# Masking the first attention with a matmul: the bf16 mask product on TensorE, maximum and difference read straight from PSUM

## The chip, the cores and the metric

One core of one Trainium2 chip runs the whole program. The metric is the device time of one execution in microseconds (us), the median of several runs. Below, TensorE is PE (PEld is its weight load), VectorE is DVE, ScalarE is ACT, GpSimd is POOL and the sync engine's queue is SP.

## What is computed

Four layers, each an attention onto a short context and a feed-forward part, both with a layernorm ahead and a tanh gate behind. The change touches only the first attention:

```python
qh, kh, vh = heads_split(q @ Wq), heads_split(k @ Wk), heads_split(v @ Wv)    # 16 heads of 64
dots = jnp.einsum('bhid,bhjd->bhij', qh, kh) * scale
dots = jnp.where(mask[:, None, :, :], -jnp.finfo(dots.dtype).max, dots)
attn = jax.nn.softmax(dots, axis=-1)
out = jnp.einsum('bhij,bhjd->bhid', attn, vh)
x = x + tanh(g) * (out.transpose(...).reshape(b, n, h * d) @ Wo + bo)
```

`x` is (4, 512, 256), the context (4, 64, 256), the mask (4, 512, 64) boolean: True hides a key. The last attention of the program (stage 6) has the same sizes, no mask, and clips the scores to [-11, 11] in place of subtracting the maximum.

## The kernel before, in words

**Stages.** The program numbers its parts 0 to 7. Stage 0 is the first attention, stage 1 an int8-valued feed-forward part in bf16, stage 6 the last attention. Each engine has its own straight list of instructions, tied to the others by counting semaphores: `pt_full`/`pt_moved` for the two PSUM buffers `pt` (transposes), `sh_full`/`sh_taken` for the two 1024-column buffers `sh` (scores), `o_full`/`o_added` for the two `ob` (outputs). The tables `PRE` and `PER` (lines 67 to 70) count the fills of each pair of buffers, so that every wait is on a known number.

**Fold (`fold16`).** Keys and values are folded with Wq and Wo beforehand: `keysA` holds, for each batch, 256 rows by 16 heads x 64 keys, so that a 128-token tile's scores for all heads are one product of 256 by 1024; `valsO` holds values times Wo. PE's product is line 695, the copies out are ACT's (lines 1181, 1183) and DVE's (lines 1494, 1505, 1512). DVE puts other work between them (the dictionary `between`): statistics of x, the row maxima of the next stage's weights, and `row_masks` (lines 1945 to 1951) at step 10. After the fold PE transposes the first normalised block (`first_norm_T`, through line 621), ACT copies it to `xnT`.

**Attention (`attend16`).** 4 batches of 4 tiles of 128 tokens, i = 0 to 15. The orders are written out by hand:

- PE in iteration i: eight transposes of the probabilities of tile i (line 621, waits on `prob_ready`), the scores of tile i+2 (line 651, into `sh`; four products of 512 columns in f32, which the trace shows as eight matmuls), the output of tile i (line 651, into `ob`; waits until ACT has moved the transposed probabilities). At the third tile of a batch the transposes of the next batch's normalised rows come first (`norm_T`), in all batches of stage 6 and in three of stage 0. In the last two iterations there are no scores.
- DVE in iteration i: `shift(i+1)`, `add(i-1)` (line 1460, output tile onto x), after a batch's last tile the statistics (lines 1406 to 1413) and in stage 0 the extremes of x (line 1528), then `normalise(i+1)` (sum line 1551, reciprocal line 1553, product line 1555), and once a batch `norm_next` (line 1419).
- ACT in iteration i: the exponential of tile i+1 (line 1193), then the two copies of the transposed probabilities of tile i (line 1130).

`shift` in stage 0 is three DVE instructions over 128 x 1024: mask times -FMAX plus scores out of PSUM into `prob` (line 1538, which frees the score buffer), maximum over the keys (line 1541), difference (line 1543). In stage 6 it is one (line 1546).

**Beside it** POOL turns the next stage's weights into integers (lines 501 to 505), two of the fourteen pieces after each batch's reciprocal root, and PE needs all fourteen right after the attention. SP starts the loads for later stages when the fold is over.

Of the kernel before, what the change touches and what calls it, by code (L numbers as in the profile page):

```python
# [52 lines left out]
QMAX = 127.0  # L53
MAGIC = 1.5 * 2.0 ** 23
FMAX = float(np.finfo(np.float32).max)
ROW = D + 2
REGION = NT * P
NSLOT = NE * REGION
# [5 lines left out]

PRE = {"pt": [2 + 2 + 4, 17 - 2, 0, 2, 0, 0, 4, 0], "sh": [20, 6, 0, 0, 0, 0, 20, 0],
       "o": [0] * 8, "ln": [1, 0, 0, 0, 0, 0, 0, 0]}
PER = {"pt": [10, 0, 3 + 4, 4, 3, 5, 10, 4], "sh": [4, 0, 1, 1, 1, 0, 4, 2],
       "o": [4, 2, 2, 2, 2, 2, 4, 2], "ln": [1, 0, 1, 1, 1, 1, 1, 1]}  # L70
# [27 lines left out]
def layers_kernel(nc, I, out):  # L98
    ctx = ExitStack()
    with ctx:  # L100
# [3 lines left out]
        def sem(name):  # L104
            return ctx.enter_context(nc.semaphore(name))
# [114 lines left out]
        wdT = area3[:, 2 * NFQ * P:3 * NFQ * P].bitcast(BF16).rearrange("p (f d) -> p f d", f=NFQ)  # L220
        sdb = area3[:, 2304:2560]
        xqT = area3[:, 6912:8960].bitcast(BF16).rearrange("p (k t) -> p k t", k=KD)
        xqi = work[:, 0:2048].bitcast(BF16)

        w1h = [area2[:, 8192 + i * 512:8704 + i * 512] for i in range(7)]
# [98 lines left out]
        sent, returned = moe_rings("sent", 2), moe_rings("returned", 2)  # L324
        fetched, y_in = moe_rings("fetched", 4), moe_rings("y_in", 4)
        gate_act = sem("gate_act")

        q_inv, q_int, q_diag = map(sem, "q_inv q_int q_diag".split())

# [271 lines left out]
        def _(pe):  # L601
# [36 lines left out]
            def T(stage, b):  # L638

                return xnT[:, (b.fill("ln", stage)[1] + 1) % 2]  # L640
# [59 lines left out]
            def attend16(stage):  # L700
                def scores(u, j):
                    n, slot = Block(u).fill("sh", stage, j)
                    sh_slot(n)
                    for c in range(2):
                        mm = product(sh[slot][:, c * 512:(c + 1) * 512],
                                     [T(stage, Block(u))[:, k, j * P:(j + 1) * P] for k in range(KD)],
                                     [keysA[:, (k * NB + u) * H * C + c * 512:(k * NB + u) * H * C + (c + 1) * 512]
                                      for k in range(KD)])
                    mm.then_inc(sh_full, 1)

                pe.wait_ge(sh_taken, start_of("sh", stage) + PRE["sh"][stage])
                scores(0, 0)
                scores(0, 1)
                for b in straight:
                    for j in range(TB):
                        next_norm = stage == 6 or b.u + 1 < NB
                        k0 = 2 * j if j < 2 or not next_norm else 2 * j + 2
                        if j == 2 and next_norm:
                            norm_T(stage, b, 4)

                        pe.wait_ge(prob_ready[stage], b.u * TB + j + 1)
                        for half in range(2):
                            n, slot = b.fill("pt", stage, k0 + half)
                            transposes(n, slot, [((P, q * P, (q + 1) * P),
                                                  prob[j % 2][:, (4 * half + q) * P:(4 * half + q + 1) * P]) for q in range(4)])
                        if j < 2:
                            scores(b.u, j + 2)
                        elif b.u + 1 < NB:
                            wait_T(stage, b.u + 1, 5)
                            scores(b.u + 1, j - 2)  # L730
                        n, slot = b.fill("o", stage, j)
                        o_slot(n)
                        pe.wait_ge(pt_moved, b.fill("pt", stage, k0 + 1)[0] + 1)
                        product(ob[slot][:, 0:D], [probT[:, m * P:(m + 1) * P] for m in range(MI)],
                                [valsO[:, (m * NB + b.u) * D:(m * NB + b.u + 1) * D] for m in range(MI)]
                                ).then_inc(o_full, 1)
# [259 lines left out]
            pe.wait_ge(pt_moved, 1)  # L996
            fold16(0, ctxT, in_wk, in_wv, in_wq, in_wo, 16)
            first_norm_T(6, 1)
            pe.wait_ge(pt_moved, 8)
            attend16(0)  # L1000


# [119 lines left out]
        def _(act):  # L1122
# [62 lines left out]

            def attend16(stage):
                def exps(i):
                    if stage == 0:
                        act.wait_ge(shifted[stage], i + 1)
                    else:  # L1190

                        act.wait_ge(sh_taken, Block(i // TB).fill("sh", stage, i % TB)[0] + 1)
                    act.activation(prob[i % 2], prob[i % 2], ACT.Exp).then_inc(exped[stage], 1)  # L1193
                exps(0)
                for b in straight:
                    for j in range(TB):
                        i = b.u * TB + j
                        if i + 1 < NT:
                            exps(i + 1)
                        next_norm = stage == 6 or b.u + 1 < NB  # L1200
                        k0 = 2 * j if j < 2 or not next_norm else 2 * j + 2
                        for half in range(2):
                            n, slot = b.fill("pt", stage, k0 + half)
                            move(n, slot, probT[:, half * 512:(half + 1) * 512])
                        if j == 1 and next_norm:
                            norm_move(stage, b, 4, stage if b.u + 1 < NB else 7)
# [103 lines left out]
            a.then_inc(pt_moved, 1)  # L1310
            fold16(0)
            first_norm_move(6, 0)
            attend16(0)

            n = start_of("pt", 1) - 2
# [81 lines left out]
        def _(dve):  # L1397
# [132 lines left out]
            def attend16(stage):  # L1530
                def shift(i):

                    b, j = Block(i // TB), i % TB
                    n, slot = b.fill("sh", stage, j)
                    dve.wait_ge(sh_full, n + 1)
                    p = prob[i % 2]
                    if stage == 0:
                        dve.scalar_tensor_tensor(heads(p), mask[:, i, :].unsqueeze(1).broadcast_to([P, H, C]), -FMAX,
                                                 heads(sh[slot][:, :]), ALU.mult, ALU.add).then_inc(sh_taken, 1)
                        dve.drain()  # L1540
                        dve.tensor_reduce(mx[:, i % 2, :], heads(p), AX.X, ALU.max)  # L1541
                        dve.drain()
                        dve.tensor_tensor(heads(p), heads(p), over_keys(mx[:, i % 2, :]), ALU.subtract).then_inc(shifted[stage], 1)  # L1543
                    else:

                        dve.tensor_scalar(p, sh[slot][:, :], -11.0, 11.0, ALU.max, ALU.min).then_inc(sh_taken, 1)

                def normalise(i):
                    p = prob[i % 2]
                    dve.wait_ge(exped[stage], i + 1)  # L1550
                    dve.tensor_reduce(sm[:, i % 2, :], heads(p), AX.X, ALU.add)  # L1551
                    dve.drain()
                    dve.reciprocal(rsm[:, i % 2, :], sm[:, i % 2, :])
                    dve.drain()
                    dve.tensor_tensor(heads(p), heads(p), over_keys(rsm[:, i % 2, :]), ALU.mult).then_inc(prob_ready[stage], 1)  # L1555

                shift(0)
                normalise(0)
                for b in straight:
                    for j in range(TB):  # L1560
                        i = b.u * TB + j
                        if i + 1 < NT:
                            shift(i + 1)
                        if i >= 1:
                            pb, pj = Block((i - 1) // TB), (i - 1) % TB
                            add(pb, stage, pj, [pj])
                            if pj == TB - 1:
                                norm_stats(pb)
                                if stage == 0:
                                    extremes(pb)  # L1570
                        if i + 1 < NT:
                            normalise(i + 1)
                        if j == 1 and (stage == 6 or b.u + 1 < NB):
                            if stage == 6 and b.u + 1 == NB:
                                dve.wait_ge(raw_split, 4)
                            norm_next(stage, b, xn_free(stage, b, 5))
                add(straight[-1], stage, TB - 1, [TB - 1])
                norm_stats(straight[-1])
                if stage == 0:
                    extremes(straight[-1])  # L1580
# [364 lines left out]
            def row_masks():  # L1945

                dve.wait_ge(in_small, 16 * 24)
                dve.tensor_copy(rowf[:, :], rowm[:, :])
                dve.drain()
                dve.tensor_scalar(rowf[:, :], rowf[:, :], 0.0, None, ALU.not_equal)  # L1950
                dve.wait_ge(gates_ready, 1)
            fold16(0, bo0, {5: lambda: first_stats(straight[0]), 8: lambda: first_stats(straight[1]), 9: first_norm,
                            10: row_masks, 13: lambda: first_stats(straight[2]), 14: lambda: row_max(0),
# [182 lines left out]
```

## Time and profile before

| what | value |
|---|---|
| time, median of 3 runs | 1038.39 us (1031.43 to 1040.41) |
| the profiled execution: its own time | 1033.12 us |
| its span, first to last instruction | 1031.0 us |
| mean granted TensorE clock | 0.888 |
| busy: PE, DVE, ACT, POOL | 79%, 66%, 32%, 30% of the span |

The span of the first attention runs from about 63 us (first scores) to about 216 us (last output added); the last attention's from about 710 us to about 846 us. A timeline row gives start, duration, engine, line, operation, destination and sources, count, and in brackets how long the engine stood idle before it and what ended that. A row with a count merges instructions that follow each other. The clock of 1.00 is 2.4 GHz, 0.50 is 1.2 GHz.

### The profile page before, as it was taken

What the parts mean: (1) busy time and instruction counts of PE and PEld (TensorE: products, weight loads), DVE (VectorE), ACT (ScalarE), POOL (GpSimd) and SP (SyncE); (2) the same over time, 40 slices, a digit from 0 to 9 for tenths busy, and PEclk for the clock granted to TensorE, in tenths of its full rate; (3) what the DMA queues carried; (4) which work ended last, traced back from release to release, by engine and by line L of the source; (5) the groups of instructions that cost most, each with busy time, mean ns of one, the idle gap of its engine ahead of it and who ended that gap; (6) DMA issues with size and microseconds to landing.
All of it is one profiled execution on the core that took longest, in us unless ns stands there. A gap on an engine that the chain in (4) does not pass through costs nothing.

```text
span 1031.0 us, 13612 instructions
## 1 busy us (share of the span) xinstructions
PE 818.2 (79%) x4182; PEld 606.4 (59%) x4184; DVE 681.5 (66%) x1791; ACT 325.9 (32%) x561; POOL 306.9 (30%) x308
## 2 busy tenths in 40 slices
PE   7679898755787678669993688977999997669992
PEld 5546566532344565559983554655666664449981
DVE  3678888863978495646647876444667546577646
ACT  2322222226822263225540211132322221315540
POOL 1055211601901154734551012200112103624550
PEclk9999999976878798779996788889999999689996
DMA  8449910000000100234424400004100001234426
GB/s 266 106 153 370 324 46 1 0 1 1 0 1 0 31 1 16 99 104 139 141 81 164 163 1 0 1 1 130 33 31 1 1 1 42 83 97 135 142 81 244
DMA packets 55475, 83.29 MB, mean 81 GB/s; under 512 B 14689, under 2 KB 44385, under 8 KB 55137
## 3 DMA queue, kind: packets, MB, share of 16 engines
q1 hardware_dynamic: 48496, 63.52, 19.7%
q0 software_dynamic: 6912, 18.95, 5.1%
q8 instruction: 35, 0.57, 0.2%
q14 instruction: 32, 0.25, 0.1%
HBM read 61.41 MB, written 37.95 MB: 96 GB/s over the span
## 4 chain that ended last, share of the span: by engine, by line
PE 51%; DVE 25%; ACT 6%; issue 6%; DVEq 6%; POOL 3%; DMA 2%; SPq 0%; POOLq 0%; ACTq 0%
PE sh L651 14%; PE ob L651 12%; PE sh L924 6%; PE ob L924 5%; PE pt L621 4%; PE pt L651 3%; DVE work L1543 2%; DVE mx L1541 2%; DVE sm L1551 2%; PE sh L695 2%; DVE xn L1419 2%; DVE x L1706 2%; DVEq L1540 2%; PE pt L916 2%; DVE stats L1406 2%
## 5 line engine op out<-in xcount | busy, mean ns | idle before, releaser
L651 PE MATMUL sh<-area,xnT 128*128 128x512 f32 (+1 forms) x384 | 138.6, 514 | 5.1 <-DVE area L1512 1.6
L482 POOL TENSOR_TENSOR rstd<-var,minush 128x4 f32<-128x4 f32 (+1 forms) x29 | 29.9, 1031 | 363.3 <-DVE var L1413 363.3
L651 PE MATMUL ob<-area,work 128*128 128x256 f32 x512 | 118.0, 384 | 10.4 <-ACT work L1130 10.4
L651 PEld LDWEIGHTS ob<-area,work 128*128 128x128 f32 x512 | 97.8, 192 | 37.9 <-issue 25.4
L557 POOL DMA_INDIRECT yt<-xn,work x80 | 76.7, 959 | 105.9 <-ACT xn L1297 93.0
L651 PEld LDWEIGHTS sh<-area,xnT 128*128 128x128 f32 x384 | 68.0, 215 | 55.2 <-issue 48.8
L1193 ACT ACTIVATE work<-work 128x1024 f32<-128x1024 f32 x32 | 33.8, 1057 | 146.6 <-DVE work L1543 94.3
L550 POOL DMA_INDIRECT xg<-area,dest x64 | 62.1, 970 | 53.4 <-DVE dest L1790 36.0
L621 PE MATMUL pt<-ident,xn 128*128 128x128 f32 x164 | 27.7, 321 | 41.1 <-DVE xn L1419 40.9
L621 PE MATMUL pt<-ident,work 128*128 128x128 f32 (+1 forms) x292 | 43.1, 291 | 20.0 <-DVE work L1555 11.6
L1551 DVE TENSOR_REDUCE sm<-work 128x16 f32<-128x1024 f32 x32 | 38.9, 1216 | 22.5 <-ACT work L1193 22.5
L1460 DVE TENSOR_TENSOR x<-ob,x 128x256 f32<-128x256 f32 x64 | 24.7, 417 | 41.7 <-PE ob L651 41.7
L621 PEld LDWEIGHTS pt<-ident,work 128*128 128x128 f32 (+1 forms) x292 | 34.1, 144 | 29.3 <-DVE work L1555 14.4
L651 PE MATMUL ob<-area 128*128 128x256 f32 (+1 forms) x152 | 42.9, 439 | 10.1 <-issue 4.5
L1130 ACT COPY work<-pt 128x512 f32<-128x512 f32 (+1 forms) x80 | 43.0, 584 | 24.4 <-PE pt L621 23.9
L651 PE MATMUL sh<-xnT,area 128*128 128x512 f32 x96 | 49.3, 669 | 0.0
L621 PEld LDWEIGHTS pt<-ident,xn 128*128 128x128 f32 x164 | 22.2, 164 | 45.3 <-DVE xn L1419 44.1
L621 PE MATMUL pt<-ident,area 128*128 128x128 f32 (+1 forms) x200 | 31.8, 302 | 21.4 <-DVE area L1419 10.2
L1406 DVE BATCH_NORM_STATS2 stats<-x 128x6 f32<-128x256 f32 x128 | 45.0, 414 | 3.0
L1142 ACT COPY xnT<-pt 128x512 f32<-128x512 f32 x44 | 24.8, 586 | 67.5 <-PE pt L621 67.5
L651 PEld LDWEIGHTS ob<-area 128*128 128x128 f32 (+1 forms) x152 | 30.5, 205 | 22.9 <-issue 9.1
L1555 DVE TENSOR_TENSOR work<-work,rsm 128x1024 f32<-128x1024 f32 x32 | 40.9, 1278 | 2.4
(287 smaller groups left out, 1743.5 us busy)
## 6 DMA issues: line engine op xcount, KB each, us to landing
work<-xg SPq DMA_DIRECT2D x80, 129.0 KB, 2.1
area<-in_L_ffn_w SPq DMA_DIRECT2D x4, 2048.0 KB, 13.1
area<-yt SPq DMA_DIRECT2D x8, 1024.0 KB, 9.2
area<-in_L_xattn_Wq SPq DMA_DIRECT2D x2, 1024.0 KB, 7.6
x<-in_x SPq DMA_DIRECT2D x1, 2048.0 KB, 15.6
area<-in_L_xattn_Wo SPq DMA_DIRECT2D x2, 1024.0 KB, 15.2
area<-in_L_xattn_Wkv SPq DMA_DIRECT2D x2, 1024.0 KB, 9.3
out<-x SPq DMA_DIRECT2D x4, 512.0 KB, 2.9
```

Of the source, the lines that this page charges most:

```text
L482: pool.tensor_tensor(rstd[:, n], var[:, n], minush[:, n], ALU.pow).then_inc(given, 1)
L550: pool.indirect_dma_start(xg_rows[:, :], bass.IndirectOffsetOnAxis(ap=dest[:, b % 2, 2 * j + w:2 * j + w + 1], axis=0), xn_rows(stage, b)[ ...
L557: pool.indirect_dma_start(yt[:, :], bass.IndirectOffsetOnAxis(ap=back_to[:, 2 * i + q:2 * i + q + 1], axis=0), ypair[i % 2][:, q * D:(q + ...
L621: mm = pe.transpose(dst[0:r, c0:c1], src, (idn or ident)[0:src.shape[0], 0:src.shape[0]])
L651: mm = pe.matmul(o, a, b, start=(k == 0), stop=(k == len(lhs) - 1))
L924: mm = pe.matmul(o, lhs[:, a, k * P:(k + 1) * P], w[:, b, bass.ds(off + k * D, D)], start=(k == 0 and t == 0), stop=(k == 1 and t == 2))
L1130: act.copy(dst, src[0:r, 0:cols_]).then_inc(pt_moved, 1)
L1142: act.copy(xnT[:, par, k, :], pt[slot][:, :]).then_inc(pt_moved, 1)
L1193: act.activation(prob[i % 2], prob[i % 2], ACT.Exp).then_inc(exped[stage], 1)
L1406: dve.bn_stats(stats[:, j, :], tile(j) if tile else xt(b, j))
L1551: dve.tensor_reduce(sm[:, i % 2, :], heads(p), AX.X, ALU.add)
L1555: dve.tensor_tensor(heads(p), heads(p), over_keys(rsm[:, i % 2, :]), ALU.mult).then_inc(prob_ready[stage], 1)
```

## The change

The mask is brought into PE's form once, on the way into the attention: DVE casts it to bf16 (`maskb`) and makes `minus_key`, a 64 x 512 matrix of eight identity blocks times `BFMAX`, the most negative bf16 number; both at step 10 of the fold. PE transposes the 16 mask tiles after `first_norm_T`, in two fills of `pt`, and ACT copies them to `maskT`. For each score tile of stage 0 and each half of 512 columns PE adds a fifth product, mask tile (64 keys by 128 tokens) times `minus_key`, in bf16, into the same accumulation. The first DVE instruction of `shift` goes; maximum and difference now read PSUM, and the score buffer is freed by the difference, for which ACT's exponential waits too. The three new tensors lie where `xqT` of the next stage is written later. `-FMAX` is replaced by the bf16 number nearest to it.

```diff
+BFMAX = -(2.0 - 2.0 ** -7) * 2.0 ** 127
-PRE = {"pt": [2 + 2 + 4, 17 - 2, 0, 2, 0, 0, 4, 0], "sh": [20, 6, 0, 0, 0, 0, 20, 0],
+PRE = {"pt": [2 + 2 + 4 + 2, 17 - 2, 0, 2, 0, 0, 4, 0], "sh": [20, 6, 0, 0, 0, 0, 20, 0],
...
+        maskT = area3[:, 6912:7936].bitcast(BF16)
+        maskb = area3[:, 7936:8448].bitcast(BF16)
+        minus_key = area3[:, 8448:8704].bitcast(BF16)
...
# PE, scores of attend16
-                        mm = product(sh[slot][:, c * 512:(c + 1) * 512],
-                                     [T(stage, Block(u))[:, k, j * P:(j + 1) * P] for k in range(KD)],
-                                     [keysA[:, ...] for k in range(KD)])
+                        lhs = [T(stage, Block(u))[:, k, j * P:(j + 1) * P] for k in range(KD)]
+                        rhs = [keysA[:, ...] for k in range(KD)]
+                        if stage == 0:
+                            lhs.append(maskT[0:C, (u * TB + j) * P:(u * TB + j + 1) * P])
+                            rhs.append(minus_key[0:C, :])
+                        mm = product(sh[slot][:, c * 512:(c + 1) * 512], lhs, rhs)
...
# PE, between first_norm_T and attend16(0)
-            pe.wait_ge(pt_moved, 8)
+            pe.wait_ge(mask_ready, 1)
+            for f in range(2):
+                transposes(8 + f, f, [((C, t * P, (t + 1) * P), maskb[:, (f * 8 + t) * C:(f * 8 + t + 1) * C]) for t in range(8)],
+                           identb, BF16)
+            pe.wait_ge(pt_moved, 10)
             attend16(0)
...
# ACT: exps waits for sh_taken in both stages; after first_norm_move
+            for f in range(2):
+                move(8 + f, f, maskT[0:C, f * 1024:(f + 1) * 1024], r=C, cols_=1024, cast=BF16)
...
# DVE, shift of attend16
                     if stage == 0:
-                        dve.scalar_tensor_tensor(heads(p), mask[:, i, :].unsqueeze(1).broadcast_to([P, H, C]), -FMAX,
-                                                 heads(sh[slot][:, :]), ALU.mult, ALU.add).then_inc(sh_taken, 1)
-                        dve.drain()
-                        dve.tensor_reduce(mx[:, i % 2, :], heads(p), AX.X, ALU.max)
-                        dve.drain()
-                        dve.tensor_tensor(heads(p), heads(p), over_keys(mx[:, i % 2, :]), ALU.subtract).then_inc(shifted[stage], 1)
+                        dve.tensor_reduce(mx[:, i % 2, :], heads(sh[slot][:, :]), AX.X, ALU.max)
+                        dve.drain()
+                        dve.tensor_tensor(heads(p), heads(sh[slot][:, :]), over_keys(mx[:, i % 2, :]),
+                                          ALU.subtract).then_inc(sh_taken, 1)
...
# DVE, row_masks (step 10 of the fold)
+                dve.tensor_copy(maskb, mask[:, :, :].rearrange("p t c -> p (t c)"))
+                dve.tensor_scalar(minus_key[0:C, :].rearrange("p (h c) -> p h c", c=C),
+                                  identb[0:C, 0:C].unsqueeze(1).broadcast_to([C, 8, C]), BFMAX, None,
+                                  ALU.mult).then_inc(mask_ready, 1)
                 dve.wait_ge(gates_ready, 1)
```

## Rows read from the trace of the kernel before

**Rows 1.** Busy by stretch: stretch, length, PE, PEld, DVE, ACT, POOL busy, clock, DMA

```profile
75.10:201.20 126.10, 115.55 (x472) 78.77 (x473) 111.19 (x147) 31.48 (x48) 46.22 (x36) 0.98 0.47 158
...
719.50:834.80 115.30, 113.46 (x480) 78.79 (x480) 72.74 (x117) 34.08 (x50) 18.86 (x11) 1.00 0.07 21
...
75.20:81.00 5.80, 5.80 (x15) 3.53 (x16) 4.51 (x4) 2.02 (x3) 5.15 (x6) 0.62 1.10 354
```

**Rows 2.** Timeline, PE's steady period in stage 0

```profile
102.03 1.04 PE L621 MATMUL pt<-ident,work 128*128 128x128 f32 x8
...
109.80 1.04 PE L621 MATMUL pt<-ident,work 128*128 128x128 f32 x8
```

**Rows 3.** Timeline, the end of the first batch

```profile
111.50 0.42 DVE L1460 TENSOR_TENSOR x<-ob,x 128x256 f32<-128x256 f32 x1
...
117.96 1.45 DVE L1555 TENSOR_TENSOR work<-work,rsm 128x1024 f32<-128x1024 f32 x1
...
119.47 1.09 PE L621 MATMUL pt<-ident,work 128*128 128x128 f32 x8 [1.75 <-DVE work L1555]
...
125.49 3.69 PE L651 MATMUL ob<-area,work 128*128 128x256 f32 x16 [1.49 <-ACT work L1130]
```

**Rows 4.** Timeline, the way into stage 0

```profile
60.97 1.04 PE L621 MATMUL pt<-ident,xn 128*128 128x128 f32 x8
...
63.55 7.11 PE L651 MATMUL sh<-area,xnT 128*128 128x512 f32 x16 [1.55 <-ACT xnT L1130]
...
67.26 1.22 DVE L1538 SCALAR_TENSOR_TENSOR work<-mask,sh 128x1024 f32<-128x1024 uint8 x1 [3.81 <-PE sh L651]
...
68.58 1.22 DVE L1541 TENSOR_REDUCE mx<-work 128x16 f32<-128x1024 f32 x1
...
75.12 1.97 PE L621 MATMUL pt<-ident,work 128*128 128x128 f32 x8 [4.46 <-DVE work L1555]
```

**Rows 5.** Timeline, the way out of stage 0

```profile
201.22 1.04 PE L621 MATMUL pt<-ident,work 128*128 128x128 f32 x8
...
205.39 5.38 PE L651 MATMUL ob<-area,work 128*128 128x256 f32 x16 [3.14 <-ACT work L1130]
...
216.19 0.42 DVE L1460 TENSOR_TENSOR x<-ob,x 128x256 f32<-128x256 f32 x1 [4.96 <-PE ob L651]
```

**Rows 6.** Groups of instructions by form, 63 to 216 us: busy, mean ns

```profile
L1543 DVE TENSOR_TENSOR work<-work,mx 128x1024 f32<-128x1024 f32 x16 | 19.9, 1241 | 1.2
L1541 DVE TENSOR_REDUCE mx<-work 128x16 f32<-128x1024 f32 x16 | 19.5, 1220 | 1.5
...
L1538 DVE SCALAR_TENSOR_TENSOR work<-mask,sh 128x1024 f32<-128x1024 uint8 x16 | 19.4, 1212 | 3.8 <-PE sh L651 3.8
```

**Rows 7.** Timeline, bf16 products of 512 columns and a bf16 copy in stage 1

```profile
247.86 1.89 PE L651 MATMUL sh<-area 128*128 x8
249.59 1.03 PE L651 MATMUL ob<-area 128*128 x4
...
235.75 0.99 ACT L1340 COPY area<-pt 128x1024 bf16<-128x1024 bf16 x1
```

**Rows 8.** Timeline, the same points in stage 6

```profile
719.49 1.09 PE L621 MATMUL pt<-ident,work 128*128 128x128 f32 x8 [1.85 <-DVE work L1555]
...
834.87 1.06 PE L621 MATMUL pt<-ident,work 128*128 128x128 f32 x8 [0.33 <-ACT xnT L1142]
...
846.39 0.42 DVE L1460 TENSOR_TENSOR x<-ob,x 128x256 f32<-128x256 f32 x1 [4.96 <-PE ob L651]
```

**Rows 9.** Timeline, after step 10 of the fold

```profile
44.82 0.59 ACT L1181 COPY area<-sh 128x512 f32<-128x512 f32 x1 [3.06 <-PE sh L695]
45.51 0.69 DVE L1505 COPY area<-sh 128x512 f32<-128x512 f32 x1 [3.02 <-ACT area L1181]
```

**Rows 10.** Timeline, POOL's last pieces for stage 1

```profile
186.84 1.04 POOL L482 TENSOR_TENSOR rstd<-var,minush 128x4 f32<-128x4 f32 x1 [28.08 <-DVE var L1413]
...
202.95 2.08 POOL L505 TENSOR_SCALAR area<-area 128x704 bf16<-128x704 f32 x1 [0.15 <-issue]
```

More of the change, by code:

```diff
@@ L326, in layers_kernel @@
         gate_act = sem("gate_act")
+        mask_ready = sem("mask_ready")
         q_inv, q_int, q_diag = map(sem, "q_inv q_int q_diag".split())
@@ L704, in scores @@
                     for c in range(2):
-                        mm = product(sh[slot][:, c * 512:(c + 1) * 512],
-                                     [T(stage, Block(u))[:, k, j * P:(j + 1) * P] for k in range(KD)],
-                                     [keysA[:, (k * NB + u) * H * C + c * 512:(k * NB + u) * H * C + (c + 1) * 512]
-                                      for k in range(KD)])
+                        lhs = [T(stage, Block(u))[:, k, j * P:(j + 1) * P] for k in range(KD)]
+                        rhs = [keysA[:, (k * NB + u) * H * C + c * 512:(k * NB + u) * H * C + (c + 1) * 512]
+                               for k in range(KD)]
+                        if stage == 0:
+                            lhs.append(maskT[0:C, (u * TB + j) * P:(u * TB + j + 1) * P])
+                            rhs.append(minus_key[0:C, :])
+                        mm = product(sh[slot][:, c * 512:(c + 1) * 512], lhs, rhs)
                     mm.then_inc(sh_full, 1)
@@ L1187, in exps @@
                 def exps(i):
[L1188 to L1192, printed above, removed]
+                    act.wait_ge(sh_taken, Block(i // TB).fill("sh", stage, i % TB)[0] + 1)
                     act.activation(prob[i % 2], prob[i % 2], ACT.Exp).then_inc(exped[stage], 1)
```

## The prediction

> **What bounds the kernel now.** I read the page's chain first: in the first attention it is almost all DVE (lines 1538, 1541, 1543, 1551, 1555) with ACT's exponential between, and only there; everywhere else it is PE or a mixture. Then I read busy time by stretch, and that warns against believing the chain alone [rows 1]: from the transposes of tile 0 to those of tile 14 the stretch is 126.1 us and DVE is busy for 111.2 of it, but PE is busy for 115.6. The two engines are nearly equally full. The reader should compare stage 6, the same PE program with one DVE instruction where stage 0 has three: 115.3 us, PE busy for 113.5 of them [rows 1]. That is what PE alone needs.
>
> The timeline says where stage 0 loses against that. Inside a batch PE already runs without a gap: transposes start at 102.03 and 109.80, a period of 7.77 us [rows 2]. The DVE loop has about the same length; the chain changes hands with hardly a loss. The losses are at the ends of batches: DVE takes 7.97 us from the add at 111.50, through statistics, extremes of x and normalising, until PE's transposes at 119.47 (1.75 us idle); the next exponential comes late behind the three-step shift, and PE's output product waits another 1.49 us [rows 3]. The first iteration is slow too: PE stood idle for 4.46 us before 75.12 [rows 4], its clock fell, and it was granted 0.62 in the next stretch [rows 1]. The same happens at the end, where 3.14 us of waiting come before an output product that then takes 5.38 us in place of 3.7 [rows 3, 5].
>
> **The change, part by part.** The sum is made against the profiled execution: span 1031.0, own time 1033.12 us.
>
> *Removed: line 1538.* 16 instructions of 1.21 us [rows 6], with the gap behind it 68.58 - 67.26 = 1.32 us per tile [rows 4], 21 us of DVE time. What the path gets from it is only what PE waits for now.
>
> *Moved: maximum and difference read PSUM.* The trace has neither in this form. Line 1538 reads 1024 f32 columns from PSUM in 1.212 us; from SBUF the maximum takes 1.220 and the difference 1.241 [rows 6]. I take no change. Bounds: 0.1 us less each (no row has DVE below 1.2 us for 1024 columns from PSUM) and, if a maximum from PSUM had to be read twice, 1.2 us more each.
>
> Here the Trainium skill speaks against the change. "Perfetto Trace Analysis", section Optimizing Scalar/DVE Operations, gives a DVE instruction about 60 ns of access overhead on SBUF and about 125 on PSUM. By that the two would take some 0.13 us more per tile; the rows above, with a PSUM reader no longer than SBUF readers, do not show it. The sum would stay what it is, since the slack worked out below is larger.
>
> *Added on PE: 2 products per tile, 28 in the loop.* In bf16 with 512 columns eight take 249.59 - 247.86 = 1.73 us, 0.216 each [rows 7]; so 0.43 us per tile, 14 iterations with scores: 6.05 us. PE is full, so nothing hides this. Lower bound: nothing, 0. Upper bound: as dear as an f32 product, two of the 16 matmuls of 7.11 us, 0.89 us each [rows 4]. I take the bf16 rows, the same type and width; loading the mask tile's weights goes beside the product before, as PEld does in general.
>
> *PE's loop.* Stage 6 goes from tile 0 to tile 14 in 834.87 - 719.49 = 115.38 us [rows 8]. 14 periods of 7.77 are 108.8, so its four `norm_T` cost 1.65 each. Stage 0 has three: 113.7. With the mask products 119.8, against 201.22 - 75.12 = 126.10 now [rows 4, 5]: 6.3 us gained.
>
> *Will DVE keep up?* Period of PE: 8.20. Inside a batch maximum, difference, exponential and normalising take 75.12 - 68.58 = 6.54 us in series [rows 4], with the add 7.0. At a batch's end PE's ob finishes, 0.2 us later the add starts, and the transposes can start 7.97 us after that [rows 3]: 8.17 against 8.20. That is a tie, so I allow 0.15 us for each of three ends, 0.4 us. The second loss (1.49 us) goes: from the transposes to the output product it was 125.49 - 119.47 = 6.02 us [rows 3]; with 1.32 less on DVE it is 4.70, and PE has scores to do until 6.02 - 1.49 + 0.43 = 4.96. Freeing the score buffer 1.3 us later costs nothing: PE asks for it one iteration later, behind transposes which need the normalised tile.
>
> *The way in.* Now the transposes end at 62.0 and scores start at 63.55 [rows 4]. New between them: 16 bf16 transposes, no longer than f32 ones (1.04 us for 8), and two ACT copies of 1024 columns, 0.99 each [rows 7], of which the first begins when its eight transposes are done: 62.4, 63.3, 64.3, 65.3. Scores start at about 65.35, 1.8 later (bounds 1.0 and 2.6). Tile 0's two mask products add 0.43, the missing instruction takes 1.32 away: tile 0's transposes at 76.05, 0.9 later than 75.12. I lose 0.9. PE's wait there becomes about 2.4 us instead of 4.46. It kept its clock at 1.85 us [rows 8] and lost it at 3.14 [rows 5]; in the sum it is kept, as in stage 6, whose 115.38 I used; if lost, it costs 2.2.
>
> *The way out.* From the transposes of tile 14 to the last add: 216.19 - 201.22 = 14.97 now [rows 5], 846.39 - 834.87 = 11.52 in stage 6 [rows 8], which has the order and almost the delays that stage 0 will have. Gain 3.45.
>
> *The preparation on DVE.* A cast of 1024 columns (at most 1.22, as line 1538, which reads the same bytes) and an instruction over 512 columns (about 0.7): 1.9 us. DVE stands idle for 3.02 us right there, and the next product's slot is only wanted when the running one ends near 44.8 [rows 9]; the copy that frees it would end at 44.4. Hidden; with the cover gone it would cost up to 1.9. Nothing else is issued: no DMA is added, and SP's loads still start at the end of the fold, `sh_taken` being the same count. POOL must finish its pieces before PE's next stage: it does so 205.03 - 186.84 = 18.2 us after the third batch's statistics [rows 10], which will come about 28 us before the end of stage 0 (two periods of 8.2 and the way out). Hidden.
>
> Sum: 6.3 + 3.45 - 0.9 - 0.4 = 8.4 us. Behind stage 0 a DVE chain takes over that starts at the last add, so all of it reaches the end: 1033.12 - 8.4 = 1024.7 us for a like execution. The runs shown have a median 5.3 us above the profiled one, so I forecast 1030.0.
>
> Here a second rule of the Trainium skill bears on the same price. "FP8 and Floating Point Precision" counts four passes through the array for true FP32; a bf16 product would then be a quarter of 0.89, 0.22 us, and the trace agrees with 0.216. It would be no longer true if PE had to empty between the two types; of this no page and no row here speaks.
>
> **Rivals.**
> *A. The forecast: PE becomes the bound*, 1030.
> *B. The mask products cost nothing on the path* (shadowed by weight loads or waits). PEld is busy for 79 of 126 us, so PE is not full of arithmetic alone; but its period is made of product times. Gain 8.4 + 6.05 = 14.5: 1024.
> *C. The gain is given back.* PE's clock stays low in the first iteration (2.2 us) and the batch ends keep about 1 us each (2.6 more): DVE is tied there to within 0.03 us, and line 1555 there ran for 1.45 us [rows 3], where line 1543 needs 1.24 for the same kind of work [rows 6]. Gain about 3.5: 1035.
> *D. Slower: the mask products are as dear as f32.* 28 x (0.89 - 0.216) = 18.9 us more, so 10.5 us slower: 1049. It decides from 0.216 + 8.4/28 = 0.52 us per product on. For it: bf16 and f32 alternate within one accumulation, which no row shows. Against: all bf16 rows of this width. A maximum that takes twice as long from PSUM comes out on the same side: its 1.2 us per tile, and 1.2 for the difference, pass the 1.3 us of slack.
> *That it doesn't do what it says*: hardly possible, line 1538 is gone from the program.
>
> **How the numbers follow.** A 0.62, B 0.10, C 0.20, D 0.08. The measurement of this kernel can tell about 1% from no change, 10.4 us. Faster by over 1%: B and the upper part of A, which lies only 2 us from that bound with a spread of the runs of 9 us: 0.27. Slower by over 1%: most of D, 0.05. Within 1%: 0.68. The range 1021 to 1037 reaches over B and C and leaves out D. A alone would be 1026 to 1034.
>
> **What would show it.** Right: the stretch between tile 0's and tile 14's transposes about 120 us long with PE busy nearly throughout; a PE period of 8.2 us in all batches; line 1541 and the difference at 1.22 to 1.25 us; the mask matmuls at 0.22; scores starting near 65.3; the last add near 208; DVE with gaps in front of the add or the shift, which it lacks now; the chain in the stage on PE. Wrong: DVE still in the chain there; a PE period at 7.8 (B) or over 9 (D); gaps of more than 0.5 us ahead of the transposes after a batch's end, or a clock of 0.6 after tile 0 (C); a change of more than 1 us in the stages behind.

## The result and the profile after

| | before | changed | ratio, 95% interval |
|---|---|---|---|
| median, first chip | 1035.72 us (18 runs) | 1039.24 us (18 runs) | 1.0038 [1.002, 1.0056] |
| median, another chip, later (experiments 5 to 8) | 1032.93 us (35 runs) | 1039.58 us (12 runs) | 1.0049 [1.0022, 1.0077] |
| the profiled execution: own time, span | 1033.12, 1031.0 us | 1040.37, 1038.6 us | |
| mean granted clock | 0.888 | 0.882 | |
| start of stage 0's last add | 216.19 us | 216.06 us | |
| from there to the end of the span | 814.8 us | 822.5 us | |

All ratios here and below are of fast runs, so that one slow run of experiment 3 (1044.9 us) and one of experiment 9 (1045.74 us) count in their medians but not in their ratios.

The forecast was 1030.0 in a range of 1021 to 1037, made from a median of 1038.39 for the kernel before; in the direct comparison that kernel had 1035.72, so that 8.4 us less would be 1027.3. It was wrong, and on the wrong side. The last two rows split the question. Stage 0 is as long as it was; of the 8.4 us it was to gain it gained 0.13. That figure is no more than scatter: from the first normalised block's transposes (`first_norm_T`) to stage 0's last add, the three profiles of the kernel before (two of them from the experiments below) took 155.2, 156.4 and 153.6 us and the four of the changed kernel 155.5 three times and 153.9. And the stages behind it, whose program is unchanged, took longer in this profile.

Busy time by stretch of the changed kernel (stretch, length, PE, PEld, DVE, ACT, POOL, clock, DMA), as in [rows 1], first from tile 0's transposes to tile 14's:

```profile
75.70:204.80 129.10, 128.03 (x500) 78.57 (x501) 96.44 (x134) 32.00 (x49) 44.56 (x34) 0.99 0.45 152
76.00:82.00 6.00, 6.00 (x17) 2.41 (x15) 4.66 (x5) 2.02 (x3) 5.35 (x6) 0.72 1.10 349
```

PE is busy for 128.0 of 129.1 us and DVE has 33 us of slack. The bound did move to PE, as forecast, but the stretch is 129 us long where the forecast had 119.8: PE is full of something that was not in the sum. Timeline of one steady iteration (start, duration, engine, line, operation), as in [rows 2]; lines 621 and 651 are 626 and 656 now:

```profile
105.21 1.04 PE L626 MATMUL pt<-ident,work 128*128 128x128 f32 x8
...
106.09 1.88 PE L656 MATMUL sh<-area,xnT 128*128 128x512 f32 x4
...
107.90 0.09 PEld L656 LDWEIGHTS sh<-area 64*128 64x128 bf16 x1 [0.76 <-issue]
107.90 0.39 PE L656 MATMUL sh<-area 64*128 64x512 bf16 x1
108.22 0.30 PEld L656 LDWEIGHTS sh<-area,xnT 128*128 128x128 f32 x2 [0.23 <-issue]
108.22 1.98 PE L656 MATMUL sh<-area,xnT 128*128 128x512 f32 x4
...
114.01 1.04 PE L626 MATMUL pt<-ident,work 128*128 128x128 f32 x8
```

The period is 114.01 - 105.21 = 8.80 us, not 8.20. Read the starts of the PEld rows against the PE rows. Among f32 products a load stands one slot (0.43 us) ahead of its product. The mask tile's load starts at 107.90, the instant its own product starts, after 0.76 us without a load; the next f32 load at 108.22 again starts with its product. The loads around the mask product are not hidden. In the chain of waits of the same iterations PE follows on itself without a gap (start, duration, what):

```profile
105.38 0.87 PE pt L626 x8
106.25 4.27 PE sh L656 x10
110.52 3.65 PE ob L656 x16
114.17 0.87 PE pt L626 x8
```

The ten matmuls of a score tile hold the chain for 4.27 us. DVE's part came as forecast. Groups by form, 60 to 216 us, against [rows 6]:

```profile
L1550 DVE TENSOR_TENSOR work<-sh,mx 128x1024 f32<-128x1024 f32 x16 | 19.6, 1225 | 1.2
L1548 DVE TENSOR_REDUCE mx<-sh 128x16 f32<-128x1024 f32 x16 | 19.5, 1221 | 16.6 <-PE sh L656 16.6
```

Maximum and difference take 1221 and 1225 ns from PSUM (1220 and 1241 from SBUF before), and DVE now waits 16.6 us in all for scores. The 60 against 125 ns of overhead that the Trainium skill gives ("Perfetto Trace Analysis", section Optimizing Scalar/DVE Operations) do not show in these durations.

The way in, as in [rows 4]:

```profile
62.05 1.05 PE L626 MATMUL pt<-identb,area 128*64 128x128 bf16 x16 [0.47 <-ACT xnT L1142]
...
64.66 1.98 PE L656 MATMUL sh<-area,xnT 128*128 128x512 f32 x4 [1.56 <-ACT area L1142]
...
75.78 1.09 PE L626 MATMUL pt<-ident,work 128*128 128x128 f32 x8 [2.12 <-DVE work L1563]
```

Scores start at 64.66 (65.35 forecast) and tile 0's transposes at 75.78 (76.05). The clock fell behind them all the same, after an idle time of only 2.12 us: 0.72 in the second window row above. The next iteration's transposes start at 86.23, so the first iteration took 10.45 us, 1.65 over the period. This is not what the kernel always does. In the changed kernel's profile with a pause of 2.3 us behind stage 0 (experiments 9 to 12) PE stands idle for the same 2.12 us, and the same six us run at full clock:

```profile
77.50:83.50 6.00, 6.00 (x21) 3.01 (x22) 4.66 (x5) 2.02 (x3) 5.35 (x6) 1.00 1.10 348
```

Its first iteration takes 86.32 - 77.47 = 8.85 us.

The way out, as in [rows 5]:

```profile
204.83 1.04 PE L626 MATMUL pt<-ident,work 128*128 128x128 f32 x8
...
216.06 0.42 DVE L1470 TENSOR_TENSOR x<-ob,x 128x256 f32<-128x256 f32 x1 [4.96 <-PE ob L656]
```

That is 11.23 us (11.52 forecast, 14.97 before). Stage 0 adds up: way in 75.78 - 75.12 = +0.66, loop (204.83 - 75.78) - 126.10 = +2.95, way out -3.74: -0.13 us. Of the way in, 0.43 us is an earlier start: `first_norm_T` begins at 60.54, against 60.97 before [rows 4]. Counted from there the way in is 15.24 us against 14.15, 1.09 longer.

### The profile page after: what moved, and what is told of

It is laid out like the page before. It is cut to its first block, busy times and chain, and to the rows that moved or that the text cites. A ratio compares the mean times of both kernels' runs of the same rounds, so it can differ in the third digit from the quotient of the medians.

```text
span 1038.6 us, 13681 instructions
## 1 busy us (share of the span) xinstructions
PE 840.7 (81%) x4230; PEld 610.8 (59%) x4232; DVE 664.2 (64%) x1777; ACT 327.8 (32%) x563; POOL 304.7 (29%) x308
## 4 chain that ended last, share of the span: by engine, by line
PE 62%; DVE 18%; issue 6%; ACT 6%; DVEq 4%; POOL 3%; DMA 2%; SPq 0%; POOLq 0%; ACTq 0%
PE sh L656 19%; PE ob L656 16%; PE sh L932 6%; PE ob L932 5%; PE pt L626 5%; PE pt L656 3%; DVE x L1714 2%; PE sh L700 2%; PE pt L924 2%; PE sh L951 2%; DVE stats L1416 1%; POOL xg L555 1%; DVE xn L1429 1%; PE sh L690 1%; DVE area L1429 1%
## 5 line engine op out<-in xcount | busy, mean ns | idle before, releaser
L656 PE MATMUL sh<-area,xnT 128*128 128x512 f32 (+1 forms) x384 | 143.5, 520 | 5.1 <-DVE area L1522 1.6
L487 POOL TENSOR_TENSOR rstd<-var,minush 128x4 f32<-128x4 f32 (+1 forms) x29 | 30.1, 1037 | 367.2 <-DVE var L1423 367.2
L656 PE MATMUL sh<-area 128*128 (+3 forms) x118 | 41.7, 473 | 16.1 <-DVE work L2040 8.3
L656 PEld LDWEIGHTS sh<-area 128*128 128x128 bf16 (+3 forms) x120 | 17.2, 147 | 53.8 <-issue 34.1
```

The lines of the kernel that those rows point to most:

```text
L487: pool.tensor_tensor(rstd[:, n], var[:, n], minush[:, n], ALU.pow).then_inc(given, 1)
L656: mm = pe.matmul(o, a, b, start=(k == 0), stop=(k == len(lhs) - 1))
```

## The experiments

Two theories for the mask product's price. T: the change of type in the PE queue costs. R: the change between weights of 64 and of 128 rows costs. A third, P, only says that the whole gain lies in the mask products' time. Experiments 1 to 4 ran on a third chip, on which the kernel before had a median of 1043.04 us (23 runs) and the changed kernel was not run. Experiments 9 to 12 ran on a fourth (before: 1032.88 us, 27 runs). Each ratio is to the kernel before on the same chip; the ratios on record differ from the quotient of the two medians by up to 0.004, so stage 0 is judged by the traces.

**1. No mask product.** What is left out: nothing is masked in this kernel.

```diff
-                        if stage == 0:
-                            lhs.append(maskT[0:C, ...])
-                            rhs.append(minus_key[0:C, :])
```

> The changed kernel without the two mask products per score tile: nothing is masked in the first attention (mask preparation, transposes and copies stay, so does the shift straight from PSUM). Theory P (price): the mask products alone took the gain, at 0.515 us each ((8.80 - 7.77) / 2), so PE's period inside a batch falls from 8.80 to 7.77 us, the last add of stage 0 comes 14 x 1.03 = 14.4 us earlier than in the changed kernel, and the kernel is about 11 us faster than before (14.8 less the 3.5 by which the changed one is slower). Theory W (waits): moving maximum and difference to PSUM, or the later release of the score buffer, costs PE something too; then the period stays above 8.0 us and the kernel is less than 6 us faster than before.

Measured: 1037.37 us, ratio 0.9918 [0.9883, 0.9952], 8.6 us by the ratio where P had about 11. Period, from the timeline:

```profile
100.62 1.04 PE L626 MATMUL pt<-ident,work 128*128 128x128 f32 x8
...
108.38 1.04 PE L626 MATMUL pt<-ident,work 128*128 128x128 f32 x8
...
116.92 1.09 PE L626 MATMUL pt<-ident,work 128*128 128x128 f32 x8 [0.61 <-DVE work L1560]
```

7.76 us, so in the changed kernel a mask product costs (8.80 - 7.76) / 2 = 0.52 us. Theory W, a cost of the moved reads beside it, is out. Stage 0's last add starts at 204.0, 12.0 us earlier than in the changed kernel, where P had 14.4. At the batch's end DVE is now late by 0.61 us: rival C's tie is real once PE is quick enough. But the whole gained less than stage 0 did; the part on the stages behind comes back to that.

**2. Both mask products first, side by side.** Two borders between mask and f32 products per tile in place of four.

```diff
+                    if stage == 0:
+                        for c in range(2):
+                            pe.matmul(sh[slot][:, c * 512:(c + 1) * 512], maskT[0:C, ...], minus_key[0:C, :], start=True, stop=False)
                     for c in range(2):
...
+                            mm = pe.matmul(..., start=(k == 0 and stage != 0), stop=(k == KD - 1))
```

> The changed kernel with both mask products of a tile issued first, one behind the other, then the four f32 products: one change from bf16 to f32 per tile in place of two there and two back. Theory T (the weight load for the product behind a change of form is not done ahead, so each border is paid): a border costs (0.515 - 0.216) / 2 = 0.15 us, four per tile become two, the period falls from 8.80 to about 8.5 us, 4.2 us less in the stage. Theory S (a 64-row bf16 product is slow by itself, 0.515 wherever it stands): the period stays at 8.80.

Measured: 1041.01 us, ratio 0.9963 [0.993, 0.9997]; its PE rows:

```profile
99.94 0.60 PE L711 MATMUL sh<-area 64*128 64x512 bf16 x2
...
107.46 1.04 PE L626 MATMUL pt<-ident,work 128*128 128x128 f32 x8
```

Its next transposes start at 115.95: a period of 8.49. Two borders gone gave back 0.31 us, 0.15 each; four borders at 0.15 are the 0.6 us by which 8.80 exceeds 8.20. The price sits in the borders, not in the product (the pair takes 0.60). Both T and R say that. Of the 4.2 us expected for the stage, the loop from tile 0 to tile 14 gave 3.7 (125.31 against 129.05); the last add, at 215.67, comes only 0.4 us earlier than in the changed kernel, because this profile's stage began later and its first score tile already ran at a granted clock of 0.71 (1.00 there in the changed kernel's).

**3. The mask in 128 rows.** Two mask tiles are transposed together into 128 rows; `minus_key` has two versions, with the identity in the upper or the lower 64 rows and zeros elsewhere. The same sums, the type still changes, the number of rows does not.

```diff
-        minus_key = area3[:, 8448:8704].bitcast(BF16)
+        minus_key = [area3[:, 8448 + 256 * i:8704 + 256 * i].bitcast(BF16) for i in range(2)]
...
-                            lhs.append(maskT[0:C, (u * TB + j) * P:(u * TB + j + 1) * P])
-                            rhs.append(minus_key[0:C, :])
+                            lhs.append(maskT[:, (u * TB + j) // 2 * P:((u * TB + j) // 2 + 1) * P])
+                            rhs.append(minus_key[j % 2])
```

> The changed kernel with 128-row mask products: the mask tiles are transposed in pairs (8 transposes of 128 x 128 in place of 16 of 128 x 64, copies of 512 columns in place of 1024), and the matrix of minus keys has its identity blocks in the upper or the lower 64 rows, zeros in the others. Order of the products as in the changed kernel, still bf16. Theory R (rows: loading 64 rows behind 128 rows cannot be overlapped): with 128 rows the load goes ahead, a mask product costs 0.216 us, the period is 8.20 and the stage 8.4 us shorter. Theory T (type: going between f32 and bf16 is what cannot be overlapped): the period stays at 8.80; only the way in gets about 1 us shorter by the smaller copies.

Measured: 1036.27 us, ratio 0.9895 [0.9843, 0.9946]. Timeline:

```profile
103.03 1.04 PE L626 MATMUL pt<-ident,work 128*128 128x128 f32 x8
...
105.20 0.10 PEld L656 LDWEIGHTS sh<-area 128*128 128x128 bf16 x1 [0.24 <-issue]
105.63 0.38 PE L656 MATMUL sh<-area 128*128 128x512 bf16 x1
...
111.23 1.04 PE L626 MATMUL pt<-ident,work 128*128 128x128 f32 x8
```

8.20 us, to the hundredth the period forecast for the change. The mask's load now starts 0.43 us ahead of its product, like any other. That is R: same types, same columns, and the whole surcharge is gone. Stage 0's last add starts at 207.9, 8.2 us earlier than in the changed kernel. Not all of that is the loop's: with half as many transposes and columns to copy, the way in from `first_norm_T` is 13.77 us in place of 15.24.

**4. The mask in f32, still 64 rows.** The counterpart: the type no longer changes, the rows do. Tiles 8 to 15 use the masks of tiles 0 to 7.

```diff
-        maskT = area3[:, 6912:7936].bitcast(BF16)
+        maskT = area3[:, 6912:7936]
...
-        minus_key = area3[:, 8448:8704].bitcast(BF16)
+        minus_key = area3[:, 8448:8960]
...
-                            lhs.append(maskT[0:C, (u * TB + j) * P:(u * TB + j + 1) * P])
+                            lhs.append(maskT[0:C, (u * TB + j) % 8 * P:((u * TB + j) % 8 + 1) * P])
...
```

> The changed kernel with the mask products in f32 and still 64 rows; tiles 8 to 15 use the masks of tiles 0 to 7. Theory T (type): with one type throughout the weight loads go ahead, an f32 product costs its two passes' 0.86 us and no more, the period is 7.77 + 1.72 = 9.5 us. Theory R (rows): the borders between 128 and 64 rows stay unhidden, 0.3 us per product, the period is 10.1 us.

Measured, in a single run: 1066.24 us.

```profile
103.59 0.29 PEld L656 LDWEIGHTS sh<-area 64*128 64x128 f32 x2 [0.76 <-issue]
103.59 1.12 PE L656 MATMUL sh<-area 64*128 64x512 f32 x2
104.64 0.30 PEld L656 LDWEIGHTS sh<-area,xnT 128*128 128x128 f32 x2 [0.76 <-issue]
...
111.17 1.04 PE L626 MATMUL pt<-ident,work 128*128 128x128 f32 x8
...
121.43 1.04 PE L626 MATMUL pt<-ident,work 128*128 128x128 f32 x8
```

A period of 10.26, where T had said 9.5 and R 10.1. With one type throughout, each border still shows 0.76 us without a load. T has fallen.

**The same border in the kernel before.** Its stage 1 already had it. At line 1065 each sum is five bf16 products of 256 columns with 128 rows and a sixth with 64, one type throughout. A row merges a 64-row load and the five 128-row loads behind it; the clock in this stretch is 1.00:

```profile
314.56 0.64 PEld L1065 LDWEIGHTS ob<-area,work 128*128 128x128 bf16 x5
315.41 0.65 PEld L1065 LDWEIGHTS ob<-area,work 64*128 64x128 bf16 x6 [0.21 <-issue]
316.27 0.66 PEld L1065 LDWEIGHTS ob<-area,work 64*128 64x128 bf16 x6 [0.21 <-issue]
```

There is 0.21 us without a load ahead of each 64-row load, and six products take 316.27 - 315.41 = 0.86 us. Six at half the 0.216 us of 512 columns [rows 7] would take 0.65, so by this estimate two changes of rows cost 0.21 us, 0.1 each. The trace of the kernel before could have told that the mask's 64 rows have a price.

The Trainium skill bears on this. "TensorEngine Tiling (Array Packing)", section Key Properties, says that changing the tiling mode drains TensorE, and its section Available Configurations counts 64 x 128 as another mode than 128 x 128. The page gives no price; these four runs agree that a change of rows has one, 0.15 us in bf16 between f32 products. The prediction found no page on emptying PE between two types. It did not ask about a change of rows, on which this page speaks.

**5. 128 rows and grouped**, experiments 2 and 3 together.

> The mask in 128 rows, and the two mask products of a tile issued first, side by side, ahead of the f32 products. Theory R (PE loses about 0.3 us wherever weights of 64 rows stand beside weights of 128): with 128 rows no border is dear, so the order is of no account: period of PE within 0.05 us of the 8.20 us of the run with 128 rows alone. Rival T (the change of type costs in itself): fewer borders would still give back 0.15 each, a period of 7.9.

Measured: 1032.54 us, ratio 0.9983 [0.9957, 1.0009]; transposes at 103.03 and 111.22, a period of 8.19. Without a change of rows the order is of no account, as R says (T had 7.9).

**6 and 7. The changed kernel and the one with 128 rows again**, on one chip.

> The changed kernel itself once more, beside the one with 128 rows on the same chip. Stage 0 has to last as long as before (last add within 0.5 us of 216.1, period 8.80). If the 3.5 us by which the medians stand apart come from behind stage 0, where the program is the same, its ratio to the kernel before may come out anywhere between 0.997 and 1.006 here; if they belong to the change, it is 1.003 to 1.005 again.

> The kernel with the mask in 128 rows once more, on the same chip as the changed kernel. From the traces stage 0 is 8.2 us shorter than in both others (last add at 207.9 against 216.1): if all of it reaches the end the ratio to the changed kernel is 0.992; the first time its ratio to the kernel before was 0.9895, 2.7 us more than stage 0 gives.

Measured: changed 1039.58, ratio 1.0049 [1.0022, 1.0077]; 128 rows 1032.83, ratio 0.9985 [0.9962, 1.0008]. Between the two medians lie 6.75 us, of the 8.2 to 9.5 by which their traces' stage 0 differs. The changed kernel's last add came at 217.9, where I had expected 216.1 within 0.5; measured from `first_norm_T`, which starts anywhere between 60.1 and 62.4 us in the profiles, stage 0 is the same 155.5 us. But against the kernel before 128 rows are no gain on this chip, with a stage 0 that ends 8 us sooner.

**8. The kernel before as a control.**

> The kernel before, unchanged, as a control: a second profile of it. Ratio 1 within its interval; stage 0 ends at 216.2 within 0.5 us; the stages behind it last between 839 and 853 us, as in the profiles so far, which tells how far one profile of them can be trusted.

Measured: 1032.96 us, ratio 1.0007 [0.998, 1.0034]; stage 0's last add at 218.8, 2.6 us later than in the first profile and outside the 0.5 us I had allowed, and 815.5 us from there to the end (I had expected 839 to 853, a range that no profile had shown).

**Where the stages behind differ.** From stage 4's last add to stage 6's first, busy time and clock; in order the kernel before, the control, the changed kernel and the changed kernel again:

```profile
605.30:727.50 122.20, 105.20 (x449) 66.66 (x448) 65.65 (x224) 28.84 (x55) 14.92 (x28) 0.89 0.11 35
```

```profile
610.60:732.20 121.60, 104.81 (x451) 66.64 (x450) 65.72 (x225) 28.84 (x55) 14.93 (x27) 0.91 0.11 35
```

```profile
606.20:732.90 126.70, 110.45 (x449) 69.50 (x448) 65.60 (x224) 28.82 (x55) 16.28 (x28) 0.85 0.11 34
```

```profile
606.60:733.30 126.70, 110.48 (x450) 69.47 (x448) 65.56 (x225) 28.84 (x55) 16.25 (x28) 0.85 0.11 34
```

The same 449 to 451 matmuls, DVE and ACT busy as before; PE is busy 5.25 us longer at a lower clock, and the stretch is 4.5 to 5.1 us longer, twice. Ten microseconds of it, kernel before and then the changed one:

```profile
630.00:640.00 10.00, 8.68 (x44) 4.84 (x44) 7.34 (x38) 1.95 (x5) 4.47 (x9) 0.97 0.00 1
```

```profile
631.00:641.00 10.00, 10.00 (x19) 4.02 (x18) 5.39 (x20) 0.57 (x1) 3.43 (x8) 0.53 0.00 0
```

One runs almost wholly at 2.4 GHz, the other at 1.2. Stage 6, where PE is busy for 114.8 of 118.9 us at a clock of 1.00, lasts 118.8 to 118.9 us from its first to its last add in every profile named here. The last stretch, behind stage 6, takes 184.5 and 183.2 us in the two profiles of before, 186.7 twice in the changed kernel's, 190.8 and 189.4 with 128 rows, 194.0 without mask products.

**9 to 12. A pause behind stage 0.** Theory L: small shifts of time decide where the low clock falls. Rival K: a fixed cost that the change leaves behind.

```diff
             dve.memset(hall[:, NFQ - 1, :], 0.0)
+            dve.drain()
+            dve.memset(hall[:, NFQ - 1, :], 0.0)
```

> The kernel before, with DVE's clearing of 2048 columns directly behind stage 0 (1.76 us in the trace of before) issued once more, with a drain between: a pause of about 1.9 us on the chain behind stage 0, stage 0 itself unchanged. Question: why do the stages behind stage 0, the same program in all kernels, last 814.7 and 815.5 us from stage 0's last add on in the two profiles of before, 822.5 and 821.0 in the two of the changed kernel and 825.5 and 828.6 with 128 rows? Theory L: where PE's low clock falls in them hangs on small shifts of time ahead of them, so a pause of 1.9 us gives any total between 5 us less and 10 us more than before plus 1.9; the 3.5 to 6 us between the medians are of this kind. Rival K: the change leaves a cost behind itself that a pause doesn't touch: this kernel then takes 1.9 us more than before, ratio 1.0018, and the stages behind last 817 us.

> The changed kernel with the same pause of about 1.9 us behind stage 0. L: its ratio to the kernel before may land anywhere between 0.997 and 1.012, and below the changed kernel's own 1.004 to 1.005 despite the added work would be a clear sign. K: 1.0055 to 1.0065, the stages behind last 823.6 us.

> The changed kernel with four such instructions more, a pause of about 7.5 us behind stage 0. L: anywhere between 1.001 and 1.016; K: 1.011 to 1.013, the stages behind last 829 us.

> The kernel with the mask in 128 rows and the pause of about 7.5 us: its stages behind stage 0 start within about 1 us of where they start in the changed kernel (207.9 + 7.5 = 215.4 against 216.1). If the start alone decided the clock behind it, they would last as in the changed kernel from there on, and the whole take about 1038.5, ratio to the changed kernel 0.999; K: as with 128 rows plus 7.5 us, 1040, ratio to before 1.006; L: neither is exact, anything within 5 us of these.

The pause is longer than I had written: in the trace each instruction with its drain takes 224.13 - 221.84 = 2.29 us, four take 9.2. By that the ratios of K become 1.0022, 1.0065, 1.0134 and 1.007.

| kernel | median | ratio, interval | behind stage 0 in the profile, less the pause |
|---|---|---|---|
| before, pause 2.3 | 1035.22 | 1.0007 [0.9976, 1.0038] | 815.1 |
| changed, pause 2.3 | 1040.2 | 1.0066 [1.0045, 1.0088] | 815.2 |
| changed, pause 9.2 | 1050.37 | 1.0158 [1.0122, 1.0193] | 823.7 |
| 128 rows, pause 9.2 | 1037.9 | 1.0018 [0.9991, 1.0045] | 821.5 |

Neither theory stands as it was put. K fits three of the four within their intervals and fails the fourth: its ratio is 0.005 below K's, its median 4 us (K: 1032.83 + 9.2 = 1042.0). There the idea that the start alone decides did well (1038.5 expected, 1037.9 measured), but other traces speak against it: counted with their pauses, the stages behind start at 218.8 in the control, 217.8 in the kernel before with a pause and 217.9 in the changed kernel again, and last 815.5, 815.1 and 821.0 us. L is right in so far as one kernel's stages behind took 815.2 us in one execution (the quickest of its eleven) and 821 to 824 in others; yet the medians scatter less freely than L allows. That quick execution shows what the others lose. Its stretch from stage 4's last add to stage 6's first is as short as in the kernel before, at the same clock:

```profile
610.10:731.80 121.70, 104.62 (x451) 66.85 (x450) 65.41 (x225) 28.81 (x55) 16.21 (x27) 0.91 0.11 35
```

**What stays open** is why the changed kernels lose their clock there more often than the kernel before. That the loss is in PE's clock is shown for the stretch above. What causes it is not: the place in time alone does not decide, as these starts show, and the denser PE work of the changed stage 0 stood ahead of the quick execution too.

## Why the prediction was wrong, by its own steps

**The failed step is the price of the mask product:** "I take the bf16 rows, the same type and width; loading the mask tile's weights goes beside the product before, as PEld does in general." It is 0.52 us, not 0.216. The rows taken were of the same type and width, but of 128 rows, and the mask tile has 64. PEld "in general" was a statement about weights of 128 rows only. (8.80 - 8.20) x 14 = 8.4 us, which is the whole forecast gain. The prediction had worked out this very point: rival D "decides from 0.216 + 8.4/28 = 0.52 us per product on". The mechanism I gave D, alternating types, was wrong (experiments 3 and 4 and line 1065 in the kernel before); its place and its threshold were right. And 0.52 lay well inside my bounds of 0 to 0.89, a range from which I kept only a small part.

**The clock in the first iteration:** "in the sum it is kept". It was lost, 1.65 us (I had priced it at 2.2). The argument rested on two rows with idle times of 1.85 and 3.14, as if idle time decided. It does not by itself: the clock behind tile 0's transposes fell after 2.12 us in three profiles of the changed kernel and stayed at 1.00 after the same 2.12 us in the fourth, and it stayed at 1.00 after 3.15 us in the one without mask products. What else decides is not shown.

**What was right.** The bound moved to PE. DVE reads PSUM at no surcharge, 1221 and 1225 ns. The way out is 11.23 for 11.52. The way in costs 1.09 for 0.9; it looks like 0.66 only by the earlier start, which is luck. Preparation on DVE is hidden and shorter than assumed:

```profile
41.83 0.69 DVE L1959 CAST area<-mask 128x1024 bf16<-128x1024 uint8 x1
42.43 0.28 DVE L1960 TENSOR_SCALAR area<-identb 64x512 bf16<-64x512 bf16 x1
```

The batch ends cost PE nothing in the changed kernel (transposes at 114.01 and 122.80, 8.79 apart), so the 0.4 us set aside for them was not needed; but only because the longer period gave DVE the room. Each `norm_T` cost (129.05 - 10.45 - 13 x 8.80) / 3 = 1.4 us in place of 1.65: stage 6's are dearer, and stage 0 of the kernel before already had 94.24 - 92.88 = 1.36. In sum: 8.4 forecast, less 8.4 for the price, less 1.65 for the clock, and back 0.75 (`norm_T`), 0.3 (way out), 0.25 (way in with the earlier start) and 0.4 (batch ends): 0.05, against 0.13 measured.

**The step behind stage 0:** "all of it reaches the end", and, as a sign of error, "a change of more than 1 us in the stages behind". The sign appeared: 7.7 us between the profiles, 3.5 to 6.6 between the medians. It is not part of my reasons for stage 0 and would have spoilt the forecast by itself: with the product at its forecast price (experiments 3, 5 and 7) stage 0's last add comes 7.8 to 8.4 us earlier than in the first profile of the kernel before, about as promised, and the ratios are 0.9895, 0.9983 and 0.9985. That this meets the 8.4 is in part luck: those kernels also have the shorter way in, which makes up for the 1.5 us that their first iteration loses by the clock.

**The best version found** is the one with 128 rows. Against the changed kernel on the same chip it is 6.75 us faster. Against the kernel before it was faster by 0.5 to 1.6% on the third chip, where that kernel was slowest, and not to be told from it on another.

## What to carry to other kernels

Price a product by rows with the same number of weight rows as well as the same type and width, and look in the trace whether its load starts a slot ahead. A short operand of 64 rows put between products of 128 is better filled up with zeros: here the columns took the same time and the borders cost nothing (8.80 to 8.20 us). Where the stages behind run at a wavering clock, judge an edit by the end of its own stage, and the whole by medians on more than one chip.

## What the runs showed of the hardware that I had not expected

- A change between weights of 64 and 128 rows keeps PE from loading ahead: 0.15 us a change in bf16 between f32 products (periods 8.80, 8.49 and 8.20 with four, two and none per tile), an estimated 0.1 between bf16 products (line 1065 of the kernel before), and about (10.26 - 7.76 - 4 x 0.43) / 4 = 0.2 us with the mask in f32 (0.43 being the slot of an f32 matmul).
- A change between bf16 and f32 products within one accumulation costs nothing that these traces show: 8.20 with four changes per tile, 8.19 with two.
- PE was granted 0.72, 0.72 and 0.71 in the six us behind an idle time of 2.12 us before tile 0, and 1.00 behind the same idle time in a fourth profile; 1.00 also behind 3.15 us (no mask products). Idle time alone does not tell whether the clock falls.
- Unchanged stages took between 814.8 us (before) and 831.6 us (no mask products) from stage 0's last add to the end; in the stretch shown it is PE's granted clock that differs, and a kernel's second profile repeated the first's length of that stretch within 0.6 us (before) and 0.1 us (changed), while a third of the changed kernel, with the pause of 2.3 us, had it 5 us shorter.
